# Two-hop graph attention on Trainium2: dense 105-word rows, one PSUM operand in the large products, and TensorE's groups reported from its own queue

## The reference

```python
def _agg(ent, rel, head, tail, etype, fc_w, fc_b):
    a_input = jnp.concatenate([ent[head], ent[tail]], axis=-1)
    e_input = jnp.sum((a_input @ fc_w.T + fc_b) * rel[etype], axis=-1)
    e = jax.nn.leaky_relu(e_input, negative_slope=0.2)
    m = jax.ops.segment_max(e, head, num_segments=n)
    exp_e = jnp.exp(e - m[head])
    denom = jax.ops.segment_sum(exp_e, head, num_segments=n)
    alpha = exp_e / denom[head]
    agg = jax.ops.segment_sum(ent[tail] * alpha[:, None], head, num_segments=n)
    return agg + ent
...
for _ in range(N_HOPS):
    ent = _agg(ent, relation_emb, head, tail, edge_type, fc_w, fc_b)
    norm = jnp.linalg.norm(ent, axis=-1, keepdims=True)
    ent = ent / jnp.maximum(norm, EPS)
...
x = _layernorm(x + _L0_gnn_ref(x, L0_gnn_relation_emb, edge_index, edge_type_20, L0_gnn_fc_w, L0_gnn_fc_b), axis=-1)
```

## Time and profile before

| | |
|---|---|
| median of 3 runs | 2910.04 us (2908.55 to 2920.16) |
| profiled execution | 2912.71 us, span 2910.3 us |
| PE, weight loads busy | 1099.4 us (38%), 839.1 us (29%) |
| DVE busy | 1850.1 us (64%) |
| ACT busy | 860.1 us (30%) |
| POOL busy | 1780.5 us (61%) |
| granted TensorE clock, mean | 0.58 of full speed |
| DMA | 265.66 MB, mean 91 GB/s |
| DMA queues' share of 16 engines | 32.4% for SP's, 10.3% for POOL's |

### The profile page before, as it was taken

One profiled execution on the slowest core, in us unless ns is written; L12 is line 12 of the kernel. 1 busy time (PEld: TensorE's weight loads), 2 busy tenths in 40 slices (PEclk: granted clock), 3 DMA queues, 4 the chain that ended last, 5 costly groups with the idle time before them and its releaser, 6 DMA issues. The chain is left out here.

```text
span 2910.3 us, 22387 instructions
## 1 busy us (share of the span) xinstructions
PE 1099.4 (38%) x4597; PEld 839.1 (29%) x4597; DVE 1850.1 (64%) x3677; ACT 860.1 (30%) x1608; POOL 1780.5 (61%) x1607
## 2 busy tenths in 40 slices
PE   4688602233233233223322634343433434333310
PEld 4577601122132123222212423221222322222210
DVE  6967863366556556556636567775776668577684
ACT  2334312454455455445521211110111111011121
POOL 1000057277777777777764347777677767767776
PEclk9556555555555555555555556565665656556555
DMA  3455432366676676676664562222222222222110
GB/s 89 124 152 151 137 61 65 61 117 105 117 127 98 115 130 114 103 121 121 100 105 95 69 127 84 67 79 65 79 67 64 81 63 80 65 66 62 55 56 13
DMA packets 235265, 265.66 MB, mean 91 GB/s; under 512 B 182810, under 2 KB 190123, under 8 KB 231636
## 3 DMA queue, kind: packets, MB, share of 16 engines
q1 hardware_dynamic: 184804, 205.51, 32.4%
q0 software_dynamic: 50416, 59.64, 10.3%
HBM read 141.54 MB, written 128.15 MB: 93 GB/s over the span
## 5 line engine op out<-in xcount | busy, mean ns | idle before, releaser
L574 POOL DMA_INDIRECT area<-tail,gi x784 | 805.6, 1028 | 294.1 <-issue 241.3
L574 POOL DMA_INDIRECT area<-head,gi x392 | 465.6, 1188 | 277.2 <-DVE gi L1138 145.2
L623 POOL DMA_INDIRECT out<-area,place x392 | 493.6, 1259 | 119.4 <-issue 119.4
L764 PE MATMUL psR<-area,row_t 128*98 128x512 f16 (+1 forms) x896 | 301.2, 518 | 634.8 <-DVE area L1186 216.4
L672 PE MATMUL psP<-V,vT 65*125 65x40 f32 (+1 forms) x1586 | 317.3, 388 | 170.1 <-issue 65.3
L764 PEld LDWEIGHTS psR<-area,row_t 128*98 128x98 f16 x896 | 157.5, 184 | 772.0 <-issue 535.2
L672 PEld LDWEIGHTS psP<-V,vT 65*125 65x125 f32 (+1 forms) x1586 | 310.0, 304 | 188.2 <-issue 70.2
L664 PE MATMUL psT<-ident,area 128*65 128x128 f32 x393 | 90.1, 420 | 560.5 <-issue 495.4
L664 PEld LDWEIGHTS psT<-ident,area 128*65 128x65 f32 x393 | 80.2, 229 | 569.0 <-issue 569.0
L869 ACT ACTIVATE area<-iota_h,half_hi 128x392 f16<-128x392 f16 x392 | 237.8, 607 | 9.4 <-issue 9.4
L1137 DVE COPY gi<-head_i 128x14 int32 (+1 forms) x28 | 5.0, 180 | 347.1 <-DMA rows<-area 299.4
(11 more groups left out here) (267 smaller groups left out, 2460.0 us busy)
## 6 DMA issues: line engine op xcount, KB each, us to landing
area<-rows SPq DMA_DIRECT2D x28, 1183.0 KB
tail<-area SPq DMA_DIRECT2D x50, 637.5 KB
area<-tail_digits SPq DMA_DIRECT2D x28, 896.0 KB
rows<-area SPq DMA_DIRECT2D x28, 735.0 KB
tail<-area SPq DMA_DIRECT2D x28, 595.0 KB
area<-tail SPq DMA_DIRECT2D x25, 637.5 KB
head<-area SPq DMA_DIRECT2D x25, 630.0 KB
area<-tail,gi POOLq DMA_INDIRECT x784
```

What stands on the lines that cost most here:

```text
L574: pool.indirect_dma_start(out=to[:, b, k, 0:tab.shape[1]], out_offset=None, in_=tab, in_offset=bass.IndirectOffsetOnAxis(ap=gi[:, b, n, k: ...
L623: pool.indirect_dma_start(out=out, out_offset=bass.IndirectOffsetOnAxis(ap=place[:, b, k:k + 1].bitcast(U32), axis=0), in_=rowO[:, b, k, 0 ...
L764: last = te.matmul(psR[g % 2][0:HH, 0:w], row_t[:, n, c, :], hot_lo[:, c, 4 * g * P:4 * g * P + w], start=c == 0 and n == 0, stop=c == HB ...
```

## The change

**Rows.** The features of the head leave the wide row. All tables have WE = 105 words (64 features, a one, 20 tail and 20 head projections): `rows0` takes the place of `tail0` and `head0`, and `rows1` (edge rows and, behind them, node rows) that of `rows1` and `tail1`. The head's features go to a table of their own, `head_xs`: ACT copies them from `rowH` to a new buffer `rowX` right behind the decays, and SP stores that. DVE's wait ahead of the indices is now for ACT's copy. SP issues one dump and one node store where it issued two, and two loads in hop 2 where it issued one. In the node stage ACT makes two copies instead of four.

**PSUM.** In hop 2 the exponentials and decays are written to PSUM (`held_ex`, `held_decay`), as are the type mask, the reciprocals, the mean, the first and last projections, the segment ends, and a copy `held` through which products and sums pass. In hop 1 small operands have copies in PSUM (`kept_...`): the reciprocals of the sum and the norm, the node scales and mean, the segment ends and the type numbers; this takes two more chained steps a chunk (36). The exponentials and decays of hop 1 stay in SBUF, and so does the sum with the head row.

**TensorE's reports.** In `transposes`, `products`, `count` and `look` the increment no longer hangs on the last matmul: PE drains and then increments from its own instruction stream. In hop 2 the sums go to `psM`, are taken within `capture` instead of at the head of the next chunk, the last of the four groups is chosen behind the chunk's last step, and `hots` waits for the groups taken instead of the sums.

```diff
@@ tables
-    tail0 = dram("tail0", [N, WT])
-    head0 = dram("head0", [NPAD, WH])
-    tail1 = dram("tail1", [NPAD + N, WT])
-    rows1 = dram("rows1", [NPAD, W1])
+    rows0 = dram("rows0", [NPAD, WE])
+    rows1 = dram("rows1", [NPAD + N, WE])
+    head_xs = dram("head_xs", [NPAD, C])
@@ SP
-            def head_x(j, b, i):
-                sp.wait_ge(s_gat[b], 16 * 2 * K * (i + 1))
+            def head_x(j, b):
+                sp.wait_ge(s_xc, j + 1)
                 sp.sem_inc(s_turn_sp, 1)
-                sp.dma_start(re[:, cols(j), X0:W1], rowH[:, b, :, 0:C]).then_inc(s_xc[b], 16)
+                sp.dma_start(xe[:, cols(j), :], rowX[:, b, :, :]).then_inc(s_xst[b], 16)
...
-                sp.dma_start(re[:, cols(j), 0:X0], rowO[:, b, :, 0:X0]).then_inc(s_dump[b], 16)
-                sp.dma_start(te[:, cols(j), :], rowO[:, b, :, 0:WT]).then_inc(s_dump[b], 16)
+                sp.dma_start(re[:, cols(j), :], rowO[:, b, :, :]).then_inc(s_dump[b], 16)
@@ POOL
-                    gather(i * 2 + b, b, 0, head0, rowH)
-                    gather(i * 2 + b, b, 1, tail0, rowT)
+                    gather(i * 2 + b, b, 0, rows0, rowH)
+                    gather(i * 2 + b, b, 1, rows0, rowT)
@@ PE, count
                     te.matmul(psC, sign_lo[:, (s0 + k) % KS, :], sign_hi[:, (s0 + k) % KS, :],
-                              start=static and t0 + k == 0, stop=True, skip_group_check=True).then_inc(s_cnt, 1)
+                              start=static and t0 + k == 0, stop=True, skip_group_check=True)
+                    pe.drain()
+                    pe.sem_inc(s_cnt, 1)
@@ PE, look
-                    last.then_inc(s_look, 1)
+                    pe.drain()
+                    pe.sem_inc(s_look, 1)
                 pe.wait_ge(s_took, j * 4 + 4)
...
-                    last = te.matmul(psX[:, k:k + 1], chosen[0:HH, k * P:(k + 1) * P], ones[0:HH, 0:1], start=True, stop=True)
-                last.then_inc(s_sum, 1)
+                    te.matmul(sums[:, k:k + 1], chosen[0:HH, k * P:(k + 1) * P], ones[0:HH, 0:1], start=True, stop=True)
+                pe.drain()
+                pe.sem_inc(s_sum, 1)
@@ ACT
-                    sc_.activation(ex[:, :, :], dl[:, :, :], ACT.Exp).then_inc(s_exp, 1)
+                    ex_, decay_ = (ex[:, :, :], decay) if h == 0 else (held_ex, held_decay)
+                    sc_.activation(ex_, dl[:, :, :], ACT.Exp).then_inc(s_exp, 1)
...
+                    if h == 0:
+                        if not static:
+                            act.wait_ge(s_xst[b], 16 * i)
+                        sc_.copy(rowX[:, b, :, :], rowH[:, b, :, 0:C]).then_inc(s_xc, 1)
@@ DVE, finish
-                link(ve.tensor_tensor(vv, agg, wide(rd[:, 0:K0], K0), ALU.mult))
-                ve.tensor_tensor(vv, vv, rowsH[:, :, 0:C], ALU.add).then_inc(s_sq, 1)
+                via, rd_, rs_, mean_ = (vv, kept_rd if kept else rd, kept_rs if kept else rs, mean) if h == 0 else (held[:, 0:K0, :], held_rd, held_rs, held_mean)
+                link(ve.tensor_tensor(via, agg, wide(rd_[:, 0:K0], K0), ALU.mult))
+                ve.tensor_tensor(vv, via, rowsH[:, :, 0:C], ALU.add).then_inc(s_sq, 1)
...
-                    link(ve.tensor_tensor(vv, vv, wide(rs[:, 0:K0], K0), ALU.mult))
-                    link(ve.tensor_tensor(vv, vv, rowsH[:, :, X0:W1], ALU.add))
+                    link(ve.tensor_tensor(via, vv, wide(rs_[:, 0:K0], K0), ALU.mult))
+                    link(ve.tensor_tensor(vv, via, rowsX, ALU.add))
@@ DVE, chunk
                         if nodes:
                             node_squares(j)
+                        if taking and h == 1:
+                            take_rows(taking[0], psM[:, 0:K])
                         if look:
                             choose(look[0], range(2))
...
                             if h == 0:
-                                dve.wait_ge(s_xc[b], 16 * (i + 1))
+                                dve.wait_ge(s_xc, j + 1)
                             indices(j + 2, b, h)
```

More of the change, by code:

```diff
@@ L253, in build_gnn @@
         psK, psY = psR
+        flatT = psT[:, :, :].rearrange("p n x -> p (n x)")
+        held = flatT[:, 0:K * C].rearrange("p (k c) -> p k c", c=C)
+        held_A = flatT[:, 0:K * R].rearrange("p (k r) -> p k r", r=R)
+        held_typ = flatT[:, K * R:2 * K * R].rearrange("p (k r) -> p k r", r=R)
+        held_part = flatT[:, 1024 - CO - 1:1024]
+        small = flatT[:, 1024:1536]
+        held_end, small = small[:, 0:T], small[:, T:]
+        held_rd, held_rs, held_mean, held_iota, held_first, held_last = (
+            small[:, a:a + n] for a, n in ((0, K), (K, K), (2 * K, K), (3 * K, R), (3 * K + R, R), (3 * K + 2 * R, R)))
+        kept_end, keep = psR[1][:, 0:T], psR[1][:, T:]
+        kept_rd, kept_rs, kept_iota = keep[:, 0:K], keep[:, K:2 * K], keep[:, 2 * K:2 * K + R]
+        kept_m, kept_r, kept_t = (keep[0:PN, 2 * K + R + n * KN:2 * K + R + (n + 1) * KN] for n in range(3))
+        assert T + 2 * K + R + 3 * KN <= 512
+        held_ex = psP[:, 1, 512 - 2 * K:512].rearrange("p (n k) -> p n k", n=2)
+        held_decay = psP[:, :, :].rearrange("p n x -> p (n x)")[:, 0:CO * (K + 1)].rearrange("p (c k) -> p c k", k=K + 1)
+        assert K * C <= 1024 - CO - 1 and 3 * K + 3 * R + T <= 512 and CO * (K + 1) <= 1024 - 2 * K
         s_src = sem("heads_loaded")
@@ L313, in build_gnn @@
         s_pr = sem("rows_projected")
[L314 to L315 removed]
+        s_xc = sem("head_x_copied")
+        s_xst = [sem(f"head_x_stored{b}") for b in range(2)]
         s_out = sem("projections_copied")
@@ L1384, in free @@
                             if h == 0:
-                                dve.wait_ge(s_xc[b], 16 * (i + 1))
+                                dve.wait_ge(s_xc, j + 1)
                             indices(j + 2, b, h)
-                    finish(h, K, b, H, r0 + j * nr, j + 1, S[:, 0:C, 1:K + 1].rearrange("p c k -> p k c"), (capture, rest), free,
-                           static and i == 0, i)
+                    finish(h, K, b, H, rowX[:, b, :, :], r0 + j * nr, j + 1, S[:, 0:C, 1:K + 1].rearrange("p c k -> p k c"), (capture, rest), free,
+                           static and i == 0, i, kept)
                     if h == 1:
                         ve.tensor_copy(place[:, b, :], write_f[:, cc]).then_inc(s_row, 1)
+                        if look:
+                            choose(look[0], range(3, 4))
                 def pair(i, static, h=h, chunk=chunk):
@@ L1397, in pair @@
                         chunk(i * 2 + b, b, static, True, i, look=(q, 1 - b, i + 1 + b) if h == 1 else None,
-                              taking=(q - 1,) if h == 1 and not (static and b == 0) else None)
+                              taking=(q - 1,) if h == 1 and not (static and b == 0) else None,
+                              kept=h == 0)
                 link.base += link.n
```

265 lines of the change are left out of this document (138 added, 127 removed).

## The result

The changed kernel took 3251.6 us (median of 4 runs, 3225.6 to 3269.2) beside 2909.3 for the kernel before (2906.3 to 2920.2): ratio 1.116, 95% interval 1.107 to 1.125. I had forecast 2555. The profiled execution's span is 3259.9 us.

What follows compares the result with a forecast made beforehand. POOL's indirect DMA issues were taken to bound the kernel: 380 us to the first gather, hop 1 1064, 78 to hop 2's first gather, hop 2 1019, 14 behind the last write, giving 2555 us; range 2480 to 2750.

Steps and rivals of the forecast that it cites:

- The sum: Whole kernel: first gather, hop 1, seam, hop 2 and what follows the last write add to 2555 us, 12% less.
- Hop 1's gathers: Hop 1: 980 us of undisturbed issues plus 28 x 3.0 of stretch, 1064 us.
- The stretch: POOL's issues lengthened beside DVE instructions: 3.0 us a chunk left in hop 1, 0.9 in hop 2.
- The seam: Between hop 1's last gathers and hop 2's first, a chain of DVE: 78 us.
- Hop 2: Gathers and writes of hop 2: 994 us of undisturbed issues plus 28 x 0.9, 1019 us.
- Part (a): DVE products with one operand in PSUM: they stretch no POOL issue; the writes' mean falls from 1259 to about 1000 ns.
- 2-port modes: Skill's claim that DVE in such a mode locks the ports, so one-hots stretch issues; rejected on one issue taking 0.95 us.
- Part (b): Dense rows and head-row copy in hop 1: indices come some 15 us earlier a chunk, POOL's 2 to 3 us pause goes.
- The cover named for the gathers' 420 bytes: DMA engines, at 0.67: the wider gathers are covered by the two tables no longer written.
- part (c): TensorE's reports by drain and own increment, sums taken 20 us later: lag between none and today's whole, taken as none.
- the 9 us: Hop 2: sums end by the model at 2222.01, DVE takes them at 2231.00; read as late completion reports of matmuls.
- The fourth rival: A POOL that never pauses holds back every report: 36 DVE steps 1.2 us slower, kernel 3000 us; chance 0.07.

Runs made afterwards that it cites:

- after, prompt: Trace of the unaltered changed kernel in a later session, where it took 2555.5 us beside 2882.1 for the kernel before.
- after, late: Trace of the same changed kernel, nothing altered, in the session where it took 3251.6 us beside 2909.3 for the kernel before.
- prompt sessions: Sessions without late reports: the unaltered changed kernel took 2555.5 and 2556.8 us, beside 2882.1 and 2814.6 for the kernel before.
- the fourth session: Session of controls; its lags are from the kernel before plus a 128x1 memset on POOL after each group of 14 issues: 2878.5 us, 1.000.
- late sessions: The two sessions in which lags were seen; the kernel before took 2908.3 and 2909.3 us, the changed kernel 3251.6 in one.
- filler: Memsets added on POOL between issues of the changed kernel, of various widths and places: 2553.8 to 2712.1 us.

## Why the prediction was right and wrong

**The sum was right, for a kernel whose reports are prompt, and its last digits are luck.** The borders of the stages in after, prompt, a timeline of POOL that answers to the earlier trace rows:

```profile
388.83 1.16 POOL L590 DMA_INDIRECT area<-rows,gi  x1 [23.89 <-DVE gi L1168]
...
1476.52 0.94 POOL L590 DMA_INDIRECT area<-rows,gi  x1 [0.30 <-issue]
...
1539.14 0.94 POOL L590 DMA_INDIRECT area<-rows,gi  x1 [0.30 <-issue]
...
2540.52 0.98 POOL L638 DMA_INDIRECT out<-area,place  x1 [0.30 <-issue]
```

- The first gather starts at 388.8; forecast 380. Hop 1's gathers take 1477.5 - 388.8 = 1089 us; forecast 1064. The stretch is 2.9 us a chunk (80 us over the plain 0.94 in 784 issues) against the 3.0 that I took. The rest is 36 us of idle time beyond the 0.30 behind each issue, 31 of them in six gaps of 3.9 to 7.2 us, one behind the first gather of every fourth chunk, without a releaser that the profile names; I had no term for them.
- The seam takes 1539.1 - 1477.5 = 61.7; forecast 78. Hop 2 takes 2541.5 - 1539.1 = 1002.4; forecast 1019. That is 8 us over the 994 of undisturbed issues, where I took 25.
- So 9 and 25 us too little stand against 16 and 17 too much, and 2555 meets 2555.5 because they cancel.
- Part (a), a product with a PSUM operand stretches nothing, is borne out by the writes' 989 ns, and its price by two kernels without drains in neighbouring sessions: operands in SBUF 2739.1, in PSUM 2547.7, 191 us. The Trainium skill's "SBUF — State Buffer", section "SBUF: two separate sides", agrees with it.
- That section's half on 2-port modes I had set aside by one row, and that reading was wrong. A one-hot takes 0.69 us. In the trace of before 24 issues start between 0.1 us ahead of a chunk's first one-hot and its end. The twelve that start up to 0.09 us behind its start take their plain 0.94 or 0.95; the one at 2231.28 is among them. The twelve that start 0.10 us or more behind it all end 1.49 to 1.57 us after its start, some 0.8 us behind its end, and so take up to 1.43. Both traces of after show the same. So the one-hots, which read a single SBUF tensor, do stretch issues, and a start within 0.09 us of theirs escapes it. The price is small, some 2 us in hop 2 of after, prompt. Timelines of DVE and POOL, before:

```profile
2535.85 2.58 DVE L1177 TENSOR_SCALAR area<-area,lo_id 128x1792 f16<-128x1792 f16 x4
...
2535.96 1.43 POOL L623 DMA_INDIRECT out<-area,place  x1 [0.30 <-issue]
```

- Part (b), with the later taking of the sums, which was never undone, is 2883.5 - 2739.1 = 144 us. L1137's wait for a DMA is gone in both traces of after. The cover named for the gathers' 420 bytes held: the DMA engines are at 0.45 in hop 1.
- DVE's cycle does fit under POOL's 35.5 us in hop 2: it is busy 161 of 200 us and POOL waits 4.0 us for an index in all of it.

**The step that failed is in part (c): I put the lag of TensorE's reports at nothing.** I wrote "below by no lag at all, above by the whole lag of today. I take the lower", on the ground that the held-back reports were completions of matmuls. The lags of the earlier trace rows were in the very trace that the argument rests on. In after, late, the drains behind the sums take 21.9 us in the middle instead of 4.0 and those behind projections up to 59.7, POOL waits 748 us for indices, and the kernel without drains takes 3116.4 in such a session. Neither end of my bounds held there: I capped the lag at "today's", up to 14.5 us behind the sums, while with a POOL of fewer stretches and pauses it reached 27.8. In the prompt sessions the drains are worth nothing either way (2547.7 and 2555.7). The Trainium skill's "TensorE: Matmul & The Clock Gate", section "The cost: per-tile semaphore tail", prices a completion increment at 26 ns. The lags of 0.04 to 0.18 us in the fourth session are nearer to it than to the 9 us that I argued from; in the late sessions the traces are far from it.

**The fourth rival had the right kind of loss and got 0.07, but its price is partly luck.** Late reports while POOL issues without a pause, and pauses of POOL in which they recover, are what after, late, shows. Its sum, however, was made of 36 steps of DVE at 1.2 us more in every second chunk, some 600 us; the trace has 129 us of such idle time in all of hop 1. The larger part is TensorE's and ACT's: the nine stands behind projections and the 218.8 us for which DVE waits for ACT. Two chunks of hop 1 take 101 us in the mean, most of them 106 to 109 with a wait of some 33 us or 91 with waits of 15.8 and 3.5, where it said 38 + 70; hop 1 lasts 1806.4 - 386.3 = 1420 us where it gave 1512. Its 3000 is short because it left hop 2 at 36.4 us a chunk. There nearly every chunk waits 9 to 17 us, behind drains and not behind DVE's steps, and hop 2 takes 3246.0 - 1876.2 = 1370 instead of 1019: 3000 - 92 + 351 = 3259, by the measured span of 3259.9. My argument against it, that the change takes out many completions, fell with the drains' 31.6 and 59.7 us; "the phase ended by itself" was true of a kernel that still stretched and paused.

**What makes a report late** is only half settled. A session of the late kind is needed; how late it gets there goes with POOL. The drains behind the sums take 21.9 us in the middle (most 31.6) with a POOL unbroken and unstretched, 9.5 (16.4) with stretched issues, 6.9 (8.7) in the kernel before with drains, which has both stretches and pauses, and 3.98 (8.2) with a pause behind every group; the times are 3251.6, 2821.8, 2928.4 and 2854.4. In the other sessions the same unbroken POOL gives 3.98 and 2547.7 to 2556.8. What makes a session late, whether the chip or something else on it or in the loading of the program, stays open: chip 1 is one case, no second session was held on it, and the run at 3251.6 may have been on it or not. Whether a filler would help there was not tried, and nor was the unaltered kernel before traced in a prompt session.

## What to carry to other kernels

Lags in a trace of before that no mechanism of the program explains may belong to where it ran: before you build on them or dismiss them, run both kernels in more than one session, and give the two outcomes as separate cases, each with its own time. Put the unaltered kernel into every group of experiments; the fillers here seemed to cure what their sessions, as far as can be told, did not have. Where late reports can occur, dense rows with operands in SBUF gave 3% in a late session (with drains) and 5% in a prompt one (without), while the full change gave 9 to 11% where reports are prompt and lost 12% where they are not.

## What the runs showed of the hardware

- In two sessions TensorE's reports came up to tens of us late while POOL issued indirect DMAs back to back (after, late: drains behind the sums median 21.9, most 31.6 us, behind projections most 59.7; 3.98 and 4.04 in after, prompt), and dependent steps of DVE stood 1.40 us apart instead of 0.21. The same kernel showed no such thing on chips 4 and 14, nor did its variants on chips 0 and 10.
- A drain with an increment by the engine's own queue does not escape this; it stops TensorE too (16.9 us ahead of 2450.48, 55.4 ahead of 1276.45).
- A DVE instruction with two SBUF tensors stretches an indirect issue that starts inside it, and so does a one-hot of 0.69 us with one: an issue that starts 0.10 us or more behind its start ends some 0.8 us behind its end, one that starts up to 0.09 us behind it takes its plain 0.94 or 0.95 (24 issues, before).
- The kernel before itself took between 2814.6 and 2909.3 us by session, 3%. Of the prompt sessions, the kernel before took 2882.1 and 2814.6 in two, 67 us apart, in which the changed one, bound by POOL's issues, took 2555.5 and 2556.8.
- A memset of 128x1 between two indirect issues costs POOL nothing: it runs within the 0.30 us that stand behind each issue (2246.57 above).
